# One image's preparation rotated over two image bodies by a table, and shifted copies made by DMA instead of VectorE

## The chip, the cores and the metric

The kernel runs on one core of one Trainium2 chip. The metric is the device time of one execution, in microseconds (us), median of the runs shown. The five engines are named as the profile names them: PE is TensorE (PEld its weight loads), DVE is VectorE, ACT is ScalarE, POOL is GpSimd, SP is SyncE, which here only issues DMAs.

## What is computed

The input is `x` of 32 images, 192 channels, 32 x 32 pixels, float32. Two residual branches follow each other.

```python
x = x + channel_attention(group_norm(x))     # 192 x 192 attention matrix per image, softmax, output product
h = group_norm(x)
offset = clip(conv3x3(h, off_w) + off_b, -8, 8)      # 2 x 9 taps
mask   = 2 * sigmoid(conv3x3(h, mask_w) + mask_b)    # 9 taps
y = deformable_conv3x3(h, offset, mask, proj_w) + proj_b   # bilinear, zero outside the image
x = x + gelu(batch_norm(y) * gamma + beta)   # mean and variance over all 32 images
```

## The kernel before

All images pass through one software pipeline. Work on an image has two parts, and every engine runs its own share of both, in program order, with semaphores between the engines.

The **body** of an image (`part1`) is 48 units, `for u in range(UNITS)`. In a unit PE does nine f16 matmuls into `acc` (`convolve`), five into `zps` for a unit ten further on (`z_group(u + AHEAD)`) and three float32 transposes into `sps` for the unit after next (`turn_s(u + 2)`). ACT copies `sps` and `zps` to f16 (`sh`, L890, and `zh`, L866), DVE forms the residues (`sl`, L1147, and `zl`, L1141), and POOL makes one `sT` tile for every two units (L1324). `sps` and `zps` have two buffers each, `sh`, `sl` and `sT` three. PE's `turn_s(v)` waits for the `sl` of v - 2, and so does `convolve`. Every twelve units PE adds `turn_y` and DVE `scale_y` (units 7, 19, ... of the body, the last after unit 47), every six ACT copies `acc`, and some units carry `y_stats` (DVE), `offset_distance` (DVE) and `column_hats` (ACT).

The **preparation** of an image (`part0`) is 48 stages, numbered 0 to 47, several of them empty. Stages 0 to 11 are statistics and the first normalisation: DVE `channel_stats` and `channel_moments` (0 to 2), `group_stats` on PE and `group_variance` on DVE (4), the power on POOL (5), four ACT normalisations (6 to 9), DVE `residue` (8 and 10). PE transposes in 12 to 15, 16 to 22 are the Gram matrix, the softmax and the products of the attention, 23 to 26 apply it and write `x1`, 27 to 29 are the second statistics, 30 to 33 four ACT normalisations into `x2`, 32 and 34 the DVE residues. Then come the copies that the 3 x 3 convolutions need:

```python
def move(k, b, par):                         # stages 33, 35 and 36, k = 0, 1, 2
    dve.tensor_copy(x2s[k] plane 0, columns 1.., <- x2 columns ..30)
    dve.tensor_copy(x2s[k] plane 1, columns ..30, <- x2 columns 1..)
    dve.tensor_copy(seam[:, 0:WRAP], src[:, H - WRAP:H])
    return dve.tensor_copy(seam[:, WRAP:2 * WRAP], src[:, 0:WRAP])
```

Stages 38 and 39 are PE's `offset_conv`, 108 matmuls each, 40 the offsets (DVE), 41 to 46 the vertical hats (DVE, ACT) and the first quarter of the horizontal hats (POOL, ACT). In the kernel before, stage u of image b + 1 stands at the end of unit u of image b on every engine; POOL, which goes by pairs of units, does stages 2p - 4 and 2p - 3 after tile p.

Image 0 is prepared alone, then image 0's body runs in straight-line code, then a hardware loop of 15 rounds with two images each, then image 31 without a preparation beside it. SP's queue holds, in order: for every image the store of `x1` and the load of the next `x` (`attended`, which waits for `x1`), and the store of `y` of the image before (`convolved`). A last phase reads `y` and `x1` back, applies the batch norm and stores the output.

Of the kernel before, what the change touches and what calls it, by code (L numbers as in the profile page):

```python
# [35 lines left out]
P = 128  # L36
# [46 lines left out]
def build(nc, x, w_qkT, w_v, w_outT, b_out, w_off, b_off, w_proj, proj_b, gamma, beta,  # L83
# [6 lines left out]
    with ExitStack() as ctx:  # L90
# [58 lines left out]

        x2s = [sb(f"x2s_{n}", [P, 2, PAD_ROWS * W], F16) for n in ("hi_a", "lo_a", "hilo_b")]  # L150

        x2w = [sb(f"x2w_{n}", [P, 2, 2 * WRAP * W], F16) for n in ("hi_a", "lo_a", "hilo_b")]

        x2 = [sb(f"x2_{n}", [P, 2, PAD_ROWS * W], F16) for n in ("hi_a", "lo_a", "hilo_b")]
        off = sb("off", [P, 2, TILES, J])
# [70 lines left out]
        x1_sb = sem("x1_sb")  # L226
        x1_stored = sem("x1_stored")
        x2_moved = sem("x2_moved")
        off_ps = sem("off_ps")
# [96 lines left out]
        def all_pairs(eng, step):  # L326
# [3 lines left out]
            for i in range(PAIRS - ROUND_ENDS):  # L330
                step(ROUNDS, i)

        def images(program, eng):

            part0, part1, weights_ready = program
            for u in range(SLOTS):
                part0(u, 0, 0)
                if u == 15:  # L340
                    weights_ready()
            part1(0, 0, True)
            with eng.Fori(1, NB - 2, 2) as b:
                part1(b, 1, True)
                part1(b + 1, 0, True)
            part1(NB - 1, (NB - 1) % 2, False)

        def image_alone(program, b, i):

            part0, part1, far_pass = program
            for u in range(SLOTS):
                part0(u, b, 0)
            part1(b, 0, False, i)
            far_pass(b, i)
# [58 lines left out]
        def _(sp):  # L415
# [30 lines left out]
            attended(0)  # L446
            with sp.Fori(1, NB - 2, 2) as b:
# [4 lines left out]
            attended(NB - 1, False)  # L452
            convolved(NB - 2)


# [18 lines left out]
            def image(b, i):  # L474
                load_x(i)
                sp.wait_ge(x1_sb, 4 * b + 4)
                store_x1(i)
                sp.wait_ge(y_final, b + 1)
                store_y(i)
# [34 lines left out]
        def _(pe):  # L514
# [227 lines left out]

            def part1(b, par, more, i=None):
                if first(b) or i is not None:
                    for g in range(AHEAD):
                        z_group(g, b, par)
                    turn_s(0, b)
                    turn_s(1, b)
                for u in range(UNITS):
                    if u + 2 < UNITS:  # L750
                        turn_s(u + 2, b)
                    elif more:
                        turn_s(u + 2 - UNITS, b + 1)
                    convolve(u, b, par)
                    if u == 9 and not more and i is None:
                        offset_max(b)
                    if u + AHEAD < UNITS:
                        z_group(u + AHEAD, b, par)
                    elif more:
# [13 lines left out]
        def _(act):  # L773
# [117 lines left out]

            def part1(b, par, more, i=None):
                if first(b) or i is not None:
                    for g in range(AHEAD):
                        split_z(g, b, par)
                    split_s(0, b)
                    split_s(1, b)
                for u in range(UNITS):
                    if u + 2 < UNITS:
                        split_s(u + 2, b)  # L900
                    elif more:
                        split_s(u + 2 - UNITS, b + 1)
                    if u % 12 == 4 and u < 36:
                        column_hats(u // 12 + 1, b, par)
                    if u % 6 == 5:
                        t = u // 6
                        act.wait_ge(sz_done, UNITS * b + u + 1)
                        if t >= 4 or not first(b):
                            act.wait_ge(yt_ps, 4 * b + t // 2 - 1)
                        act.copy(ypm[:, t % 4, 0:C], acc[:, 0:C])  # L910
                        act.copy(ypm[:, t % 4, C:2 * P], acc[:, P:C]).then_inc(y_pm, 1)  # L911
                    if u + AHEAD < UNITS:
                        split_z(u + AHEAD, b, par)
                    elif more:
                        split_z(u + AHEAD - UNITS, b + 1, 1 - par)
                    if more:
                        part0(u, b + 1, 1 - par)

# [17 lines left out]
        def _(dve):  # L936
# [64 lines left out]

            def move(k, b, par):

                rows = lambda v: v.rearrange("p (h w) -> p h w", w=W)
                src = rows(inner(x2[k], par))
                dve.tensor_copy(rows(inner(x2s[k], 0))[:, :, 1:W], src[:, :, 0:W - 1])
                dve.tensor_copy(rows(inner(x2s[k], 1))[:, :, 0:W - 1], src[:, :, 1:W])
                seam = rows(x2w[k][:, par])
                dve.tensor_copy(seam[:, 0:WRAP], src[:, H - WRAP:H])
                return dve.tensor_copy(seam[:, WRAP:2 * WRAP], src[:, 0:WRAP])  # L1010

            def zero_outside(hat, rows, tiles):
# [10 lines left out]
            def part0(u, b, par):  # L1023
# [55 lines left out]
                if u == 32:  # L1079
                    residue(0, inner(x2[1], par), inner(x2[0], par), 1, b)  # L1080
                if u == 33:
                    if not first(b):
                        dve.wait_ge(off_ps, b)
                    move(0, b, par)
                if u == 34:
                    residue(1, inner(x2[2], par)[CB:P], inner(x2[2], par)[CB:P], 1, b)
                if u == 35:
                    dve.wait_ge(xn_lo, 4 * b + 4)
                    move(1, b, par)
                if u == 36:  # L1090
                    move(2, b, par).then_inc(x2_moved, 1)
                if u == 40:
# [122 lines left out]

            def part1(b, par, more, i=None):
                if first(b) or i is not None:
# [4 lines left out]
                for u in range(UNITS):  # L1222
                    if u + 2 < UNITS:
                        split_s(u + 2, b)
                    elif more:
                        split_s(u + 2 - UNITS, b + 1)
                    if u + AHEAD < UNITS:
                        split_z(u + AHEAD, b, par)
                    elif more:
                        split_z(u + AHEAD - UNITS, b + 1, 1 - par)  # L1230
                    if u == 7 and i is None:
                        offset_distance(b, par)
                        if not more:
                            offset_flag_wanted()
                    if u == 11 and i is None and not more:
                        offset_flag()
                    if 5 <= u < 7 and i is None and not first(b):
                        y_stats(u - 3, b - 1, 1 - par)
                    if u in (38, 39) and i is None:
                        y_stats(u - 38, b, par)  # L1240
                    if u % 12 == 7 and u > 12:
                        scale_y(u // 12 - 1, b, par)
                    if more:
                        part0(u, b + 1, 1 - par)
                scale_y(3, b, par)
                if not more and i is None:
                    y_stats(2, b, par)
# [31 lines left out]
        def _(pool):  # L1279
            pool.memset(mhalf[:, :], -0.5)  # L1280
            pool.memset(minus[:, :], -1.0)
            for t in (*x2, *x2s):
                ins = pool.memset(t[:, :, :], 0.0)
            ins.then_inc(pool_setup, 1)
# [26 lines left out]

            def part1(b, par, more, i=None):
                for p in range(3 * TILES):
# [12 lines left out]
                    if p in (1, 4, 10):  # L1326
                        column_distance((1, 4, 10).index(p) + 1, b, par)
                    if more:

                        for u in (2 * p - 4, 2 * p - 3):  # L1330
                            part0(u, b + 1, 1 - par)

# [60 lines left out]
```

## Time and profile before

| | |
|---|---|
| time, median of 3 runs | 4050.97 us (4041.22 to 4051.61) |
| the profiled execution | 4042.66 us, span 4041.0 us |
| PE busy | 3563.3 us, 88% of the span |
| DVE busy | 2633.4 us, 65% |
| ACT busy | 2109.1 us, 52% |
| POOL busy | 1412.3 us, 35% |
| mean granted PE clock | 0.961 |

The body of image 0 begins at 122.8 us and that of image 31 ends about 3817 us. What lies behind it, some 220 us, is the last phase, which is bound by DMA and which the change doesn't touch. In a profile line the part in front of the bar is busy time, the part behind it idle time before the instructions and what ended it.

### The profile page before, as it was taken

To read this page: it belongs to the slowest core of one execution; us is meant where nothing else is said; L and a number is where in the kernel's file an instruction comes from. 1 tells how busy PE (TensorE), PEld (TensorE's weight loads), DVE (VectorE), ACT (ScalarE), POOL (GpSimd) and SP (SyncE) were. 2 spreads that over 40 slices of the span, in tenths; PEclk is the share of its full clock that TensorE was granted. 3 is DMA by queue.
4 is the path that set the end of the run, shared out by engine and by line. 5 is a ranking of instruction groups with operands and counts; after the bars stand their busy time and mean duration, and the time that the engine had idled before them with its cause. 6 is when DMAs were issued, how large, how long until landed. Compare 5 with 4: busy or idle time off the path is not lost.

```text
span 4041.0 us, 108743 instructions
## 1 busy us (share of the span) xinstructions
PE 3563.3 (88%) x38307; PEld 3052.9 (76%) x38307; DVE 2633.4 (65%) x5773; ACT 2109.1 (52%) x4790; POOL 1412.3 (35%) x1165
## 2 busy tenths in 40 slices
PE   3999999999999999999999999999999999999700
PEld 2788887888888788888878888887887878788700
DVE  3566776676667667676766766676666667766622
ACT  1555554555555455555545555555555555555432
POOL 1333333343433333333333333333333333333311
PEclk8999999999999999999999999999999999999955
DMA  2000000000000000000000000000001000000299
GB/s 63 20 10 28 29 28 20 28 28 18 20 28 28 20 28 28 28 10 28 28 21 28 28 28 10 29 28 28 20 28 28 28 11 28 28 20 18 69 374 322
DMA packets 50763, 170.48 MB, mean 42 GB/s; under 512 B 9665, under 2 KB 10881, under 8 KB 50177
## 3 DMA queue, kind: packets, MB, share of 16 engines
q1 hardware_dynamic: 39584, 136.75, 11.1%
q0 software_dynamic: 7168, 25.17, 1.6%
q8 instruction: 349, 5.72, 0.6%
q14 instruction: 238, 1.94, 0.2%
q10 hardware_dynamic: 3424, 0.90, 0.1%
HBM read 87.29 MB, written 75.50 MB: 40 GB/s over the span
## 4 chain that ended last, share of the span: by engine, by line
PE 62%; DVE 14%; issue 11%; ACT 5%; DMA 4%; DVEq 2%; ACTq 1%; SPq 1%; POOL 0%; POOLq 0%
PE sps L680 9%; PE acc L697 6%; PE acc L699 6%; PE acc L698 6%; PE l L609 4%; DVE zl L1141 3%; PE zps L666 3%; PE zps L670 3%; PE zps L667 3%; PE zps L668 3%; PE zps L669 3%; DVE sl L1147 2%; DMA xn<-x_scratch 2%; ACT sh L890 2%; DVE ych L1201 2%
## 5 line engine op out<-in xcount | busy, mean ns | idle before, releaser
L1324 POOL TENSOR_TENSOR sT<-ay,bx 128x768 f32<-128x768 f32 x768 | 1149.1, 1506 | 1400.8 <-PE sps L680 1333.5
L1147 DVE TENSOR_TENSOR sl<-sps,sh 128x384 f16<-128x384 f32 x1536 | 846.8, 551 | 597.9 <-ACT sh L890 595.0
L697 PE MATMUL acc<-zh,sh 128*128 128x192 f16 x4608 | 1139.7, 247 | 0.3 <-ACT ypm L911 0.3
L698 PE MATMUL acc<-zl,sh 128*128 128x192 f16 x4608 | 1139.7, 247 | 0.0
L699 PE MATMUL acc<-zh,sl 128*128 128x192 f16 x4608 | 1139.7, 247 | 0.0
L890 ACT CAST sh<-sps 128x384 f16<-128x384 f32 x1536 | 740.5, 482 | 728.4 <-PE sps L680 723.5
L866 ACT CAST zh<-zps 128x288 f16<-128x288 f32 x1536 | 619.7, 403 | 652.5 <-PE zps L670 625.5
L680 PE MATMUL sps<-eye,sT 128*128 128x128 f32 x4608 | 790.9, 281 | 155.7 <-DVE sl L1147 96.1
L1141 DVE TENSOR_TENSOR zl<-zps,zh 128x288 f16<-128x288 f32 x1536 | 693.4, 451 | 356.9 <-ACT zh L866 351.8
L680 PEld LDWEIGHTS sps<-eye,sT 128*128 128x128 f32 x4608 | 536.1, 142 | 308.5 <-DVE sl L1147 168.9
L698 PEld LDWEIGHTS acc<-zl,sh 128*128 128x128 f16 x4608 | 453.6, 98 | 18.5
L697 PEld LDWEIGHTS acc<-zh,sh 128*128 128x128 f16 x4608 | 453.5, 98 | 1.1 <-DVE sl L1147 0.5
L699 PEld LDWEIGHTS acc<-zh,sl 128*128 128x128 f16 x4608 | 453.5, 98 | 0.5
L666 PE MATMUL zps<-wpr_h,x_hi_a 128*128 128x288 f16 x1344 | 387.2, 288 | 1.2 <-DVE zl L1141 0.7
L667 PE MATMUL zps<-wpr_l,x_hi_a 128*128 128x288 f16 x1344 | 386.9, 288 | 0.0
L668 PE MATMUL zps<-wpr_h,x_lo_a 128*128 128x288 f16 x1344 | 386.4, 287 | 0.0
L669 PE MATMUL zps<-wpr_h,x_hilo_b 128*128 128x288 f16 x1344 | 385.8, 287 | 0.0
L670 PE MATMUL zps<-wpr_l,x_hilo_b 128*128 128x288 f16 x1344 | 385.7, 287 | 0.0
L1308 POOL TENSOR_TENSOR bx<-off,cx_sb 128x576 f32<-128x576 f32 x128 | 155.5, 1215 | 458.8 <-DVE off L1104 458.8
L1290 POOL TENSOR_TENSOR rstd<-gvar,mhalf 128x2 f32<-128x2 f32 x64 | 44.9, 702 | 563.5 <-DVE gvar L994 563.5
L609 PE MATMUL l<-wof,x2s_hi_a 128*128 128x54 f16 x1536 | 182.6, 186 | 9.8 <-DVE x2w_hilo_b L1010 9.8
L609 PE MATMUL l<-wof,x2s_lo_a 128*128 128x54 f16 x1536 | 182.5, 186 | 0.0
(201 smaller groups left out, 6466.3 us busy)
## 6 DMA issues: line engine op xcount, KB each, us to landing
xin<-in_x SPq DMA_DIRECT2D x32, 512.0 KB, 5.3
xin<-in_x SPq DMA_DIRECT2D x64, 256.0 KB, 5.9
x_scratch<-x SPq DMA_DIRECT2D x32, 512.0 KB, 2.8
y_scratch<-ych SPq DMA_DIRECT2D x32, 512.0 KB, 2.7
zh<-y_scratch SPq DMA_DIRECT2D x20, 512.0 KB, 10.9
zl<-x_scratch SPq DMA_DIRECT2D x20, 512.0 KB, 12.4
out<-zh POOLq DMA_DIRECT2D x20, 512.0 KB, 8.8
x_scratch<-x SPq DMA_DIRECT2D x32, 256.0 KB, 3.5
```

Of the source, the lines that this page charges most:

```text
L609: mm = pe.matmul(o, src[:, row * W:(row + ROWS_T) * W], wof[:, m, k].rearrange("p i j -> p (i j)"), start=(k == 0 and n == 0), stop=(k == ...
L666: pe.matmul(o, at(0), wpr_h[:, 0, ky, n], start=True, stop=False)
L667: pe.matmul(o, at(0), wpr_l[:, 0, ky, n], start=False, stop=False)
L680: mm = pe.transpose(sps[u % 2][:, kx * P:(kx + 1) * P], sT[:, g, kx, c * P:(c + 1) * P], eye32[:, :])
L697: pe.matmul(acc[:, 0:C], s_h, zh[:, j, ky, z], start=start and kx == 0, stop=False)
L698: pe.matmul(acc[:, 0:C], s_h, zl[:, j, ky, z], start=False, stop=False)
L699: mm = pe.matmul(acc[:, 0:C], s_l, zh[:, j, ky, z], start=False, stop=stop and kx == 2)
L866: act.copy(z_piece(zh, g, par), zps[:, g % 2, 0:KO // 2]).then_inc(z_hi, 1)
L890: act.copy(sh[:, u % S_RING].rearrange("p k n -> p (k n)"), sps[u % 2][:, 0:3 * P]).then_inc(s_hi, 1)
L1141: dve.tensor_tensor(z_piece(zl, g, par), zps[:, g % 2, 0:KO // 2], z_piece(zh, g, par), ALU.subtract)\
L1147: dve.tensor_tensor(one(sl), sps[u % 2][:, 0:3 * P], one(sh), ALU.subtract).then_inc(s_lo, 1)
L1324: pool.tensor_tensor(sT[:, p % ST_RING].rearrange("p k (r x) -> p k r x", r=R), a, x_, ALU.mult)\
```

## The change

1. The three planes of `x2`, `x2s` and `x2w` become one tile each, with the plane as a dimension.
2. DVE's `move` goes (twelve copies per image). SP issues four SBUF-to-SBUF DMAs in its place (`shift`), each of 128 partitions x 3 planes: two of 96 elements (192 bytes) per run, two of 1023 elements (2046 bytes) per run. The planes are now shifted as a flat row, and POOL clears the column that wrapped (`edges`, two memsets in stage 37), which releases PE's `offset_conv` and, for the next body, `z_group`.
3. A table `PLAN` says in which unit each stage stands. Stages 0 to 18 of image b + 2 stand in units 30 to 47 of image b, stages 19 to 46 of image b + 1 in units 0 to 29 of image b. Between stage 34 (unit 16) and stages 35 to 37 (unit 20) there are three units without a stage. Image 0's body takes the whole of image 1's preparation in 38 units and stages 0 to 18 of image 2 in the last ten.
4. The loop has 14 rounds, and images 29, 30 and 31 stand behind it.
5. `column_hats` moves from units 4, 16, 28 to 4, 14, 22, `offset_distance` from 7 to 17, `y_stats` from 5, 6, 38, 39 to 2, 3, 35, 37.

```diff
+        PLAN = {-18: (0,), -17: (1,), -16: (2,), -15: (3,), -14: (4,), -13: (5,),
+                -12: (6,), -11: (7,), -10: (8,), -9: (9,), -8: (10, 11), -7: (12,), -6: (13,), -5: (14,), -4: (15,),
+                -3: (16,), -2: (17,), -1: (18,), 0: (19,), 1: (20,), 3: (21,), 4: (22,), 5: (23,), 6: (24,),
+                7: (25,), 8: (26,), 9: (27,), 10: (28,), 11: (29,), 12: (30,), 13: (31,), 14: (32,), 15: (33,),
+                16: (34,), 20: (35, 36, 37), 21: (38,), 22: (39,), 23: (40,), 24: (41,), 25: (42,), 27: (44,),
+                28: (45,), 29: (46,)}
+        LEAD = -min(PLAN)
+        FIRST_UNITS = UNITS - 10
+        def squeezed(units, span, offset):
+            out = {}
+            for at in range(span):
+                out.setdefault(offset + at * units // span, []).extend(PLAN.get(at - LEAD, ()))
+            return out
+        FIRST_PLAN = squeezed(FIRST_UNITS, LEAD + max(PLAN) + 1, 0)
+        FIRST_LEAD = squeezed(UNITS - FIRST_UNITS, LEAD, FIRST_UNITS)
+        def beside(part0, u, b, par, left):
+            if left >= 1:
+                for stage in FIRST_PLAN.get(u, ()) if first(b) else PLAN.get(u, ()) if u >= 0 else ():
+                    part0(stage, b + 1, 1 - par)
+            if left >= 2:
+                for stage in FIRST_LEAD.get(u, ()) if first(b) else PLAN.get(u - UNITS, ()):
+                    part0(stage, b + 2, par)
...
-            with eng.Fori(1, NB - 2, 2) as b:
+            with eng.Fori(1, NB - 4, 2) as b:
...
+            def shift(b, par):
+                sp.wait_ge(xn_lo, 4 * b + 4)
+                plane = x2_all[:, :, par, PAD_T * W:PAD_T * W + N]
+                flat_plane = lambda h: x2s_all[:, :, h, PAD_T * W:PAD_T * W + N]
+                sp.dma_start(x2w_all[:, :, par, 0:WRAP * W], plane[:, :, N - WRAP * W:N]).then_inc(x2_shifted, 16)
+                sp.dma_start(x2w_all[:, :, par, WRAP * W:2 * WRAP * W], plane[:, :, 0:WRAP * W])\
+                  .then_inc(x2_shifted, 16)
+                sp.dma_start(flat_plane(0)[:, :, 1:N], plane[:, :, 0:N - 1]).then_inc(x2_shifted, 16)
+                sp.dma_start(flat_plane(1)[:, :, 0:N - 1], plane[:, :, 1:N]).then_inc(x2_shifted, 16)
...
             with sp.Fori(1, NB - 2, 2) as b:
                 attended(b)
+                shift(b, 1)
                 convolved(b - 1)
                 attended(b + 1)
+                shift(b + 1, 0)
                 convolved(b)
...
-                if u == 33:
-                    if not first(b):
-                        dve.wait_ge(off_ps, b)
-                    move(0, b, par)
...
-                if u == 35:
-                    dve.wait_ge(xn_lo, 4 * b + 4)
-                    move(1, b, par)
-                if u == 36:
-                    move(2, b, par).then_inc(x2_moved, 1)
...
+                if u == 37:
+                    edges(b)
...
+            def edges(b):
+                pool.wait_ge(x2_shifted, 64 * b + 64)
+                pool.sem_inc(edges_due, 1)
+                for h in range(2):
+                    rows = x2s_all[:, :, h, PAD_T * W:PAD_T * W + N].rearrange("p k (r w) -> p k r w", w=W)
+                    ins = pool.memset(rows[:, :, :, (W - 1) * h:(W - 1) * h + 1], 0.0)
+                ins.then_inc(x2_moved, 1)
...
-                    if more:
-                        part0(u, b + 1, 1 - par)
+                    beside(part0, u, b, par, left)
```

## Rows read from the trace of the kernel before

**Rows 1.** The page: busy time by engine; the SP queue: packets, MB, share of 16 engines.

```profile
PE 3563.3 (88%) x38307; PEld 3052.9 (76%) x38307; DVE 2633.4 (65%) x5773; ACT 2109.1 (52%) x4790; POOL 1412.3 (35%) x1165
...
q1 hardware_dynamic: 39584, 136.75, 11.1%
```

**Rows 2.** One instruction per image (stage 40): duration, first and last start in us.

```profile
L1097 DVE SCALAR_TENSOR_TENSOR off<-l,unscale,boff x32: 431/433/443, 106.4 to 3729.1; 128x216 f32<-128x216 f32 x32
```

**Rows 3.** Waits of PE from 320 to 3720 us: total us, times, longest.

```profile
PE sps L680 <- DVE sl L1147: 91.3, 119, 1.1
PE sps L680 <- issue: 48.4, 14, 3.7
PE l L540 <- DVE gram L1057: 17.4, 29, 0.6
```

**Rows 4.** PE's timeline, the transposes of `turn_s` in units 33 to 37: start, us.

```profile
2066.95 0.49 PE L680 MATMUL sps<-eye,sT 128*128 128x128 f32 x3
2068.64 0.49 PE L680 MATMUL sps<-eye,sT 128*128 128x128 f32 x3
2070.61 0.55 PE L680 MATMUL sps<-eye,sT 128*128 128x128 f32 x3
2073.59 0.55 PE L680 MATMUL sps<-eye,sT 128*128 128x128 f32 x3 [1.08 <-DVE sl L1147]
2075.80 0.55 PE L680 MATMUL sps<-eye,sT 128*128 128x128 f32 x3 [0.31 <-DVE sl L1147]
```

**Rows 5.** DVE's timeline over the same units.

```profile
2068.38 1.72 DVE L1000 TENSOR_TENSOR x_lo_a<-xn,x_hi_a 128x1024 f16<-128x1024 f32 x1
...
2071.53 1.45 DVE L1009 COPY x2w_hi_a<-x_hi_a 128x96 f16<-128x96 f16 x1
...
2073.93 1.22 DVE L1000 TENSOR_TENSOR x_hilo_b<-xn,x_hilo_b 64x1024 f16<-64x1024 f32 x1
```

**Rows 6.** POOL's timeline over the same units.

```profile
2071.24 1.69 POOL L1324 TENSOR_TENSOR sT<-ay,bx 128x768 f32<-128x768 f32 x1 [2.23 <-PE sps L680]
```

**Rows 7.** ACT's timeline, `sh` before and behind the normalisation of stage 31.

```profile
2065.23 0.47 ACT L890 CAST sh<-sps 128x384 f16<-128x384 f32 x1
...
2067.02 0.48 ACT L890 CAST sh<-sps 128x384 f16<-128x384 f32 x1
```

**Rows 8.** PE's timeline, the transposes that end units 9, 10 and 11.

```profile
2007.47 0.49 PE L680 MATMUL sps<-eye,sT 128*128 128x128 f32 x3
2009.45 0.55 PE L680 MATMUL sps<-eye,sT 128*128 128x128 f32 x3
2011.19 0.49 PE L680 MATMUL sps<-eye,sT 128*128 128x128 f32 x3
```

**Rows 9.** DVE's timeline, the residue of stage 10.

```profile
2010.94 1.70 DVE L1000 TENSOR_TENSOR xhl_b<-xn,xhl_b 64x1024 f16<-64x1024 f32 x1
```

**Rows 10.** PE's timeline, units 42 to 44, 46, and `turn_y` in 47.

```profile
2093.40 0.49 PE L680 MATMUL sps<-eye,sT 128*128 128x128 f32 x3
2095.86 0.55 PE L680 MATMUL sps<-eye,sT 128*128 128x128 f32 x3 [0.61 <-DVE sl L1147]
2097.86 0.55 PE L680 MATMUL sps<-eye,sT 128*128 128x128 f32 x3
...
2101.33 0.49 PE L680 MATMUL sps<-eye,sT 128*128 128x128 f32 x3
2103.26 0.32 PE L710 MATMUL yt<-eye,ypm 128*128 128x128 f32 x1
```

**Rows 11.** Groups by line, ACT: one half of `column_hats`.

```profile
L857 ACT ACTIVATE bx<-bx 128x576 f32<-128x576 f32 x128 | 88.5, 691 | 0.1
```

**Rows 12.** Groups by line, DVE: one half of `scale_y`.

```profile
L1201 DVE TENSOR_SCALAR ych<-yt,unscale,pb 128x256 f32<-128x256 f32 x256 | 126.2, 534 | 2.3 <-PE yt L711 2.3
```

**Rows 13.** DMA issues: KB each, median us from issue to landing.

```profile
xin<-in_x SPq DMA_DIRECT2D x64, 256.0 KB, 5.9
x_scratch<-x SPq DMA_DIRECT2D x32, 512.0 KB, 2.8
```

More of the change, by code:

```diff
@@ L148, in build @@
         rinv = sb("rinv", [P, 2])
-        x2s = [sb(f"x2s_{n}", [P, 2, PAD_ROWS * W], F16) for n in ("hi_a", "lo_a", "hilo_b")]
-        x2w = [sb(f"x2w_{n}", [P, 2, 2 * WRAP * W], F16) for n in ("hi_a", "lo_a", "hilo_b")]
-        x2 = [sb(f"x2_{n}", [P, 2, PAD_ROWS * W], F16) for n in ("hi_a", "lo_a", "hilo_b")]
+        x2s_all = sb("x2s", [P, 3, 2, PAD_ROWS * W], F16)
+        x2w_all = sb("x2w", [P, 3, 2, 2 * WRAP * W], F16)
+        x2_all = sb("x2", [P, 3, 2, PAD_ROWS * W], F16)
+        x2s, x2w, x2 = [[t[:, k] for k in range(3)] for t in (x2s_all, x2w_all, x2_all)]
         off = sb("off", [P, 2, TILES, J])
@@ L477, in image @@
                 store_x1(i)
+                shift(b, 0)
                 sp.wait_ge(y_final, b + 1)
@@ L741, in far_pass, with part1 @@
                     mm.then_inc(fyt_ps, 1)
-            def part1(b, par, more, i=None):
+            def part1(b, par, left, i=None):
                 if first(b) or i is not None:
@@ L751, in part1 @@
                         turn_s(u + 2, b)
-                    elif more:
+                    elif left:
                         turn_s(u + 2 - UNITS, b + 1)
                     convolve(u, b, par)
-                    if u == 9 and not more and i is None:
+                    if u == 9 and not left and i is None:
                         offset_max(b)
@@ L758, in part1 @@
                         z_group(u + AHEAD, b, par)
-                    elif more:
+                    elif left:
                         z_group(u + AHEAD - UNITS, b + 1, 1 - par)
@@ L900, in part1 @@
                         split_s(u + 2, b)
-                    elif more:
+                    elif left:
                         split_s(u + 2 - UNITS, b + 1)
-                    if u % 12 == 4 and u < 36:
-                        column_hats(u // 12 + 1, b, par)
+                    if u in (4, 14, 22):
+                        column_hats((4, 14, 22).index(u) + 1, b, par)
                     if u % 6 == 5:
@@ L913, in part1 @@
                         split_z(u + AHEAD, b, par)
-                    elif more:
+                    elif left:
                         split_z(u + AHEAD - UNITS, b + 1, 1 - par)
-                    if more:
-                        part0(u, b + 1, 1 - par)
+                    beside(part0, u, b, par, left)
             images((part0, part1, lambda: None), act)
@@ L1000, in residue @@
                 dve.tensor_tensor(lo, xn[:, 0] if i == 0 else xn[CB:P, 1], hi, ALU.subtract).then_inc(xn_lo, 1)
[L1002 to L1010, printed above, removed]
             def zero_outside(hat, rows, tiles):
@@ L1214, in y_stats, with part1 @@
                     ins.then_inc(y_final, 1)
-            def part1(b, par, more, i=None):
+            def part1(b, par, left, i=None):
                 if first(b) or i is not None:
@@ L1224, in part1 @@
                         split_s(u + 2, b)
-                    elif more:
+                    elif left:
                         split_s(u + 2 - UNITS, b + 1)
@@ L1228, in part1 @@
                         split_z(u + AHEAD, b, par)
-                    elif more:
+                    elif left:
                         split_z(u + AHEAD - UNITS, b + 1, 1 - par)
-                    if u == 7 and i is None:
+                    if u == (17 if left else 7) and i is None:
                         offset_distance(b, par)
-                        if not more:
+                        if not left:
                             offset_flag_wanted()
-                    if u == 11 and i is None and not more:
+                    if u == 11 and i is None and not left:
                         offset_flag()
[L1237 to L1240, printed above, removed]
+                    if u in (2, 3) and i is None and not first(b):
+                        y_stats(u, b - 1, 1 - par)
+                    if u in (35, 37) and i is None:
+                        y_stats((u - 35) // 2, b, par)
                     if u % 12 == 7 and u > 12:
                         scale_y(u // 12 - 1, b, par)
-                    if more:
-                        part0(u, b + 1, 1 - par)
+                    beside(part0, u, b, par, left)
                 scale_y(3, b, par)
-                if not more and i is None:
+                if not left and i is None:
                     y_stats(2, b, par)
@@ L1281, in _ @@
             pool.memset(minus[:, :], -1.0)
-            for t in (*x2, *x2s):
-                ins = pool.memset(t[:, :, :], 0.0)
+            for t in (x2_all, x2s_all):
+                ins = pool.memset(t[:, :, :, :].rearrange("p k h n -> p (k h n)"), 0.0)
             ins.then_inc(pool_setup, 1)
@@ L1327, in part1 @@
                         column_distance((1, 4, 10).index(p) + 1, b, par)
-                    if more:
-                        for u in (2 * p - 4, 2 * p - 3):
-                            part0(u, b + 1, 1 - par)
+                    for u in (2 * p - 4, 2 * p - 3):
+                        beside(part0, u, b, par, left)
+                for u in range(UNITS - 4, UNITS):
+                    beside(part0, u, b, par, left)
             images((part0, part1, lambda: None), pool)
```

20 lines of the change are left out of this document (13 added, 7 removed).

## The prediction

> **What bounds the kernel now.** I read the page first: PE is busy 88% of the span, DVE 65% [rows 1], so the body of the images is PE's, and a gain must be PE time that is not work. Stage 40 comes once per image, from 106.4 to 3729.1 us over 31 intervals: 116.9 us per image [rows 2]. The waits of PE in the steady stretch are few: the transposes of `turn_s` wait for DVE's `sl`, 3.1 us per image; 14 waits of some 3.5 us are for nothing but issue, one at each turn of the loop; and one product of stage 21 waits 0.6 us for DVE [rows 3].
>
> A wait in that list is counted short, because the last matmul's end covers its beginning. So I measure from start to start. A quiet unit takes 1.68 us (two `turn_s` in a row are 1.69 apart), and then come 1.97, 2.98 and 2.21 us [rows 4]; the next unit, with `move(1)`, repeats the 2.98. These four units lie where stages 33 to 36 stand. The surplus is 0.29 + 1.30 + 0.53 + 1.30 = 3.4 us per image, the largest stall outside the loop turn.
>
> The reader should see why. DVE's seam copy of 96 elements takes 1.45 us [rows 5] and ends at 2072.98, with the POOL tile that began at 2071.24 and took 1.69 (to 2072.93) [rows 6]: the copy sat behind POOL. By the Trainium skill ("SBUF — State Buffer", section Terms) DVE and GpSimd share a port pair that is locked for a full instruction; the trace agrees, and the sum is the same with or without that rule. In the same way the residue of stage 34 is 1.22 us and that of stage 32 1.72 us [rows 5].
>
> **How much lateness is free.** `turn_s(v)` needs the `sl` of v - 2, so an `sl` may be about one unit, 1.68 us, later than in a quiet unit before PE stands still; PE work that lies between (a `turn_y`, a stage) adds to that. ACT has its own: with a normalisation in the unit one `sh` follows the other by 1.79 us [rows 7], 0.11 more than a unit, so four in a row are just affordable. These two facts size every new collision below.
>
> **The change, part by part.** Per image beside which a full preparation runs:
>
> *The moves go*: -3.4. Their wait behind POOL goes too. DVE is then idle in the units that held them.
>
> *Stage 21* is now two units behind stage 20 instead of one: the product's wait goes. It is 0.6 idle; corrected as above (1.08 idle [rows 4] against 1.30 by starts) about -0.75.
>
> *Stages 8 to 12.* Before, the unit that follows the residue of stage 8 takes 1.98 us [rows 8], 0.30 over; in the new place a `turn_y` (some 0.4 us of PE work) lies there and hides it: -0.3. But stage 12 follows stage 10 by one unit instead of two. The residue of stage 10 ends at 2012.64 [rows 9]; one unit earlier PE would come to its transposes at about 2011.2 [rows 8]. PE would wait 1.4 us; if the residue runs without POOL's tile in its way, in 1.22 as stage 34's, 0.9. Bounds 0.9 and 1.5, I take +1.4. Behind the waiting transposes all of PE is queued.
>
> *Stages 41 to 46.* Before, two units take 2.46 and 2.00 [rows 10], 1.1 over, since ACT's hats hold up `sh`. A `turn_y` now falls in the first of them: -0.4, the rest stays. Stage 46's unit has no `turn_y` behind it any more and body unit 47 has stage 18 in front of its own: the 0.25 by which `turn_y` waited (2103.26 - 2101.33 - 1.68) [rows 10] go. `column_hats` at 22 lies beside stage 39, a long PE unit; at 4 beside stage 22, likewise. Both at nothing, and 0.5 if that cover failed.
>
> *column_hats in unit 14* lies among the four normalisations. It adds 2 x 0.69 = 1.4 us of ACT [rows 11] to an `sh` already 1.1 late (the interval of 1.79 [rows 7] less `sh` and `zh` themselves, an estimate), less 0.4 for the `turn_y` of unit 14: 2.1 against a free 1.68 is a stall of 0.45, and with the residue of stage 32 [rows 5] queued on DVE behind it up to 1.0, of which 0.3 were there before. Net +0.1 to +0.7; I take +0.4, as DVE's part depends on POOL's timing.
>
> *scale_y in unit 31* now lies before stages 1 and 2 and puts 2 x 0.53 us [rows 12] in front of the moments for which PE's stage 4 waits. DVE had some 0.6 us to spare per unit (1.68 less a `sl` and a `zl`). 0 to 1.06, I take +0.45.
>
> *The transfer.* SP is free at unit 16 (the `x1` store and `x` load go out at unit 8, the `y` store at unit 3), so nothing is queued behind `shift` for ten units. The four DMAs move 2 x 786 KB and 2 x 74 KB, 1.72 MB. The SP queue moved 136.75 MB in 11.1% of sixteen engines' time over 4041 us [rows 1], that is 305 KB/us with all sixteen busy. A 512 KB store lands in 2.8 us [rows 13], of which 1.7 would be data: 1.1 fixed. So 1.1 + 5.6 = 6.7 us. From below: at the store's own whole rate less a fixed 1.5, 400 KB/us, 5.8. From above: three loads, 1.05 MB, the last issued about 1.5 us behind the first and landing 5.9 later [rows 13], 7.4; scaled, 11.4. I take 6.7, nearer the stores since nothing is read from HBM. `edges` on POOL adds about 0.5 (an estimate; no row shows so small a strided memset; under the 1.69 of a whole tile [rows 6]). Together 7.2. What covers it: from the residue's end, about 2.3 us into unit 17 counted on DVE's lag (the 1.22 of [rows 5] behind its `zl`), to `offset_conv` at the end of unit 21: some 3.3 units, 5.6 us. PE waits +1.6 us; bounds 0.7 and 6.3. POOL waits too, in program order, with tile 12 done: tile 13 is needed at unit 24, behind both `offset_conv`, so that wait costs nothing below some 8 us more.
>
> By the Trainium skill ("DMA: Bandwidth & Descriptors", section Anatomy of one DMA, a fit for the path over GpSimd) a DMA takes about 2.0 us + bytes/436 KB per us; that estimate would be 5.9 us and 0.8 less stall. The same page of the Trainium skill (section Specifications) wants 512 B for line rate, which speaks against the 192-byte seam runs; doubling their 0.15 MB would add about half a microsecond. No run so far shows either for SBUF to SBUF.
>
> *Sum per image*: removed 3.4 + 0.75 + 0.3 + 0.4 + 0.25 = 5.1; added 1.4 + 0.4 + 0.45 + 1.6 = 3.85. Net -1.25 us, times about 29 = -36.
>
> *Once*: one loop turn fewer, -3.5, and less slow PE after it. In the preparation of image 0 nothing hides the transfer: 7.2 against the moves behind its second residue, about 2.5: +5. Image 0's body packs 48 + 18 stages into 48 units: in its last ten units two stages of a chain share a unit six times, and 35 to 38 share one four units behind 34 instead of five. At one to two us for each that is about +13. The fewer rounds leave more straight-line code; at nothing, since the trace shows no issue wait on entering or leaving the loop.
>
> *Total*: -36 - 3.5 + 5 + 13 = -21 against the profiled 4042.7: 4021. The median of the runs is 0.2% above the profiled time, which would make it 4030; I forecast 4026, between the two.
>
> **The rivals.**
>
> *B, more is hidden.* The transfer lands in 5.8 and the planes' residues run at 1.22: no wait at unit 21 (-1.6) and 0.5 less at unit 41. For it: everything at the quick end is in a row above. Against it: it needs the cover of 5.6 to hold. -2.1 x 29 = -61: about 3965.
>
> *C, the transfer is slow: slower than before.* 384 runs per DMA instead of 128, shifted by two bytes, could go at the loads' pace. With 11.4 us `offset_conv` starts 4.7 us later: +136, about 4160. It decides from where the net gain is gone: 25 us over 29 images is 0.9, so from about 7.6 us for the four DMAs; by 0.3% slower from 8.0. Waits of over 3 us would also be like the loop turns', of which the mean granted clock of 0.961 has its share. Midway, 9 us, gives about 4095.
>
> *D, crowding.* Every unit now has a stage, and DVE and ACT are late more often than my list has it. One more us per image: about 4055, no change.
>
> **How the numbers follow.** A, my forecast, 4026 with its own range 3995 to 4050: 0.40. B, 3940 to 3995: 0.22. C, over 4063: 0.23. D, 4040 to 4063: 0.15. A measurement of this kernel can tell 0.3%, 12 us, from no change: faster is below 4039. Faster: 0.36 of A, B and a little of D, 0.6; same: the rest of A and D, 0.16; slower 0.24. The range 3945 to 4100 leaves out the ends of B and C.
>
> **What would show it.** No DVE copies at the old lines; in units 16 to 20 `turn_s` 1.68 apart; PE's stage 38 waiting for POOL's memset 1 to 2 us, and 5.8 to 7.5 us from the first of SP's four DMAs to the last landing; PE's stage 12 waiting 1 to 1.5 for DVE's residue; `turn_s` in units 14 to 17 at most 1 us late; stage 40 every 115.6 us. Wrong if the DMAs take over 8 us, if stage 12 finds its residue done, or if image 0's body takes over 20 us more than the 117 or so of the others.

## The result: slower by 3.3%

The changed kernel takes 4181.95 us (median of 4 runs, 4178.28 to 4185.12) against 4051.29 us: a ratio of 1.033, 95% interval 1.031 to 1.035. One of the four runs behind the 4051.29 is a slow one of 4744.94 us, which the ratio leaves out; without it the median is the 4050.97 given above. Forecast were 4026 us and a range up to 4100. In the profiled execution the span is 4176.2 us against 4041.0.

The page of the changed kernel, busy time by engine and the SP queue, and its stage 40 once per image (answers to [rows 1, 2]):

```profile
PE 3591.9 (86%) x38307; PEld 3083.9 (74%) x38307; DVE 2482.4 (59%) x5389; ACT 2098.3 (50%) x4790; POOL 1413.4 (34%) x1225
...
q1 hardware_dynamic: 90784, 191.76, 14.6%
```
```profile
L1124 DVE SCALAR_TENSOR_TENSOR off<-l,unscale,boff x32: 432/433/443, 109.3 to 3821.9; 128x216 f32<-128x216 f32 x32
```

DVE lost 151 us of work, as the change meant it to, and PE is busy for a smaller share: the gain on DVE was not PE's. PE's waits from 320 to 3720 us (total, times, longest), beside [rows 3]:

```profile
PE l L657 <- POOL x2s L1338: 81.2, 29, 3.3
PE sps L728 <- DVE sl L1174: 55.6, 114, 1.2
PE sps L728 <- issue: 53.8, 26, 2.6
PE l L601 <- DVE xhl_b L1046: 37.8, 28, 1.4
```

The first line is the wait for the transfers and POOL's `edges`, 2.8 us per image, and it is new. So is the fourth, stage 12 behind the residue of stage 10, 1.35 us. The waits for `sl` fell from 3.1 to 2.0 us, not to nothing. One wait for the transfers in time, on SP, POOL and PE:

```profile
2122.51 0.69 SPq L479 DMA_DIRECT2D x2w<-x  x1
...
2124.61 0.64 SPq L483 DMA_DIRECT2D x2s<-x  x1
```
```profile
2129.72 0.93 POOL L1338 MEMSET x2s<- 128x96 f16 x2 [8.50 <-DMA x2s<-x]
```
```profile
2130.71 0.32 PE L657 MATMUL l<-wof,x2s 128*128 128x54 f16 x3 [2.32 <-POOL x2s L1338]
...
2134.93 0.53 PE L728 MATMUL sps<-eye,sT 128*128 128x128 f32 x3
...
2136.64 0.24 PE L657 MATMUL l<-wof,x2s 128*128 128x54 f16 x3
...
2139.37 0.53 PE L728 MATMUL sps<-eye,sT 128*128 128x128 f32 x3
```

SP issues the four one after the other, 0.7 us each, so the two large ones (`x2s`) are issued 1.4 and 2.1 us behind the first. From the first issue to POOL's start it is 7.2 us, and 8.2 to PE's.

This is the shorter of two kinds, which alternate from image to image: of the 29 waits 14 are 2.3 us long and 14 are 3.3. In the longer kind, as behind the first issue at 2246.52, POOL starts 8.2 us behind it, and the DMA view of 2246.5 to 2255 us has one packet of instructions among those of the four transfers:

```profile
2254.70 0.93 POOL L1338 MEMSET x2s<- 128x96 f16 x2 [9.47 <-DMA x2s<-x]
```
```profile
q14 instruction: 1, 0.01, 0.2%
```

The same view of 2122.5 to 2130 has none. It is like that in every run that kept this order of the transfers: without such a packet the four land in 7.0 to 7.5 us, with one in 7.1 to 9.2, most often about 8.0. No run changes this packet alone, so that it is the cause is likely and not shown.

Now compare the two halves of the convolution, 108 matmuls each: the first takes 4.2 us (2130.71 to 2134.93), the second 2.7 (2136.64 to 2139.37). The same image by stretches (busy us of PE, PEld, DVE, ACT and POOL, granted PE clock, DMA share, GB/s):

```profile
2128.40:2130.70 2.30, 0.00 (x0) 0.00 (x0) 0.46 (x1) 0.40 (x1) 0.98 (x3) 1.00 0.32 124
2130.70:2135.00 4.30, 4.29 (x109) 4.29 (x110) 0.00 (x0) 0.00 (x0) 2.57 (x2) 0.60 0.01 4
2135.00:2141.00 6.00, 6.00 (x146) 5.75 (x143) 1.49 (x3) 2.75 (x7) 0.00 (x0) 1.00 0.01 3
```

Behind 2.3 us without a matmul PE was granted 0.60 of its clock, that is 1.2 GHz instead of 2.4 for most of the stretch. It fell so behind 20 of the 29 waits, 9 of the 14 short ones and 11 of the 14 long ones. Before the change it fell, in this stretch of 320 to 3720 us, only behind the loop's turn.

To see where the rest went I took the start of each of the 48 units from the trace and compared its mean over images 2 to 28 with a unit of the same content that has no stall. What stands over, us per image, before and after:

| place | before | after | forecast of the difference |
|---|---|---|---|
| the moves, units 35 to 37 | 3.1 | 0 | -3.4 (with unit 34) |
| stage 21 | 0.9 | 0.1 | -0.75 |
| offset convolution: wait and slow clock | 0.1 | 3.9 | +1.6 |
| stages 8 to 12 | 0.5 | 1.9 | +1.1 |
| four normalisations, residues (16 to 18; before 34) | 0.3 | 1.2 | +0.4 |
| stages 41 to 46 | 1.2 | 2.0 | -0.4 |
| stage 4 | 0.2 | 0.7 | +0.45 |
| loop turn and slow clock behind it | 2.7 | 3.2 | 0 |
| stage 28, `turn_y` in 47 | 0.9 | 0.6 | -0.25 |
| all | 9.9 | 13.6 | -1.25 |

Measured whole, a body takes 117.0 us before and 120.6 after, and the bodies of images 1 to 29 together 100 us more. The turn's share rose because PE now waits twice there, 4.1 us in all, where it waited once for 3.5. Once per execution: image 0's body takes 143.9 us instead of 114.1, of which 10 are work that image 30 no longer has (104.0 instead of 114.3), so +20; the preparation of image 0 +3; the last phase +12. The last is not the change's: in the padded kernel before (below) it takes 236 us, as in the changed one, against 224 in the profile of before.

### The profile page after: what moved, and what is told of

Read it like the earlier page. It is cut to its first block, busy times and chain, and to the rows that moved or that the text cites. A ratio compares the mean times of both kernels' runs of the same rounds, so it can differ in the third digit from the quotient of the medians.

```text
span 4176.2 us, 107654 instructions
## 1 busy us (share of the span) xinstructions
PE 3591.9 (86%) x38307; PEld 3083.9 (74%) x38307; DVE 2482.4 (59%) x5389; ACT 2098.3 (50%) x4790; POOL 1413.4 (34%) x1225
## 4 chain that ended last, share of the span: by engine, by line
PE 57%; DVE 13%; issue 10%; DMA 8%; ACT 5%; SPq 2%; DVEq 2%; ACTq 2%; POOL 1%; POOLq 0%
PE sps L728 8%; PE acc L745 5%; PE acc L746 5%; PE acc L747 5%; PE l L657 5%; DMA x2s<-x 4%; PE zps L718 3%; PE zps L714 3%; PE zps L715 3%; PE zps L716 3%; PE zps L717 3%; DVE zl L1168 2%; DMA xn<-x_scratch 2%; DVE x L1046 2%; DVE sl L1174 2%
## 5 line engine op out<-in xcount | busy, mean ns | idle before, releaser
L1361 POOL TENSOR_TENSOR sT<-ay,bx 128x768 f32<-128x768 f32 x768 | 1137.5, 1492 | 1343.8 <-PE sps L728 1340.2
L728 PE MATMUL sps<-eye,sT 128*128 128x128 f32 x4608 | 791.7, 281 | 118.8 <-DVE sl L1174 61.2
L728 PEld LDWEIGHTS sps<-eye,sT 128*128 128x128 f32 x4608 | 545.6, 142 | 210.8 <-DVE sl L1174 108.9
L714 PE MATMUL zps<-wpr_h,x 128*128 128x288 f16 x1344 | 386.7, 288 | 0.4
L718 PE MATMUL zps<-wpr_l,x 128*128 128x288 f16 x1344 | 386.6, 288 | 0.0
L715 PE MATMUL zps<-wpr_l,x 128*128 128x288 f16 x1344 | 386.6, 288 | 0.0
L716 PE MATMUL zps<-wpr_h,x 128*128 128x288 f16 x1344 | 386.6, 288 | 0.0
L717 PE MATMUL zps<-wpr_h,x 128*128 128x288 f16 x1344 | 386.6, 288 | 0.0
L657 PE MATMUL l<-wof,x2s 128*128 128x54 f16 x4608 | 214.7, 194 | 105.9 <-POOL x2s L1338 105.9
L657 PEld LDWEIGHTS l<-wof,x2s 128*128 128x128 f16 x4608 | 197.6, 102 | 117.0 <-POOL x2s L1338 115.4
```

The costliest lines, as they stand in the source:

```text
L657: mm = pe.matmul(o, src[:, row * W:(row + ROWS_T) * W], wof[:, m, k].rearrange("p i j -> p (i j)"), start=(k == 0 and n == 0), stop=(k == ...
L714: pe.matmul(o, at(0), wpr_h[:, 0, ky, n], start=True, stop=False)
L715: pe.matmul(o, at(0), wpr_l[:, 0, ky, n], start=False, stop=False)
L728: mm = pe.transpose(sps[u % 2][:, kx * P:(kx + 1) * P], sT[:, g, kx, c * P:(c + 1) * P], eye32[:, :])
L1361: pool.tensor_tensor(sT[:, p % ST_RING].rearrange("p k (r x) -> p k r x", r=R), a, x_, ALU.mult)\
```

## The experiments

Each is compared with the kernel before on the same chip; ratios carry their 95% interval. The kernel before took 4041 to 4047 us beside the experiments and 4051 beside the changed kernel, so a difference of under some 10 us between two groups of experiments says little by itself. Numbers per unit are taken as for the table.

**The two halves of the change.** First the transfers alone, with `PLAN` = `{u: (u,)}` and hats, `offset_distance` and `y_stats` in their old units.

> The four transfers and POOL's edges as in the change, but every stage, column_hats, offset_distance and y_stats back in their old units (stage u in unit u). Theory (the wait for the transfers, and the slow clock behind it, is the largest part of the loss): the cover is about 4 us here for 8.2 us from the residue's end to the edges, so PE waits about 4 us in unit 38 and its offset convolution runs about 1.5 us longer; the moves' 3.1 us are saved. +2.5 us per image, about 4125 us. Rival (the new places of the stages cost, the transfers are hidden): 3.1 us less per image than before, about 3960 us.

4183.1 us, 1.0335 (1.0318 to 1.0353). The direction is the theory's, the size is 58 us more. Its largest wait of PE:

```profile
PE zps L709 <- POOL x2s L1333: 150.1, 28, 6.3
```

5.4 us per image, and not at the convolution: `z_group` of the next image also waits for `x2_moved`, and with the stages in their old units it comes first in unit 38. I had overlooked it. With the slow clock, unit 38 is 7.2 us over. Another 7 us that the expectation left out come once per execution, in the preparation of image 0, where no body hides the transfers.

Then the table alone: `move(0)` to `move(2)` back on DVE in units 15, 17 and 18, without `shift` and `edges`.

> The table with DVE's copies in place of transfers and edges: move(0) in unit 15, move(1) in 17, move(2) in 18. Theory: the wait in unit 21 goes (-3.8 us per image against the change), the moves' stall comes back (3.1 to 4 us), the other new stalls and the long first body stay: 4165 to 4190 us, as slow as the change. Rival (the transfers are the whole loss): the table by itself is neutral, about 4050 us.

4129.2 us, 1.020 (1.018 to 1.022): better than the 4165 to 4190 expected. The moves in their new places stall PE by 2.9 us and not 3.1 to 4, and without transfers the preparation and the body of image 0 take 12 us less, which the expectation left out; some 20 us of the difference stay open. But it is 82 us slower than before. So each half alone makes the kernel slower; the transfers are not the whole loss.

**The wait.** Stages 35 to 46 two units later:

```diff
-16: (34,), 20: (35, 36, 37), 21: (38,), 22: (39,), 23: (40,), 24: (41,), 25: (42,), 27: (44,), 28: (45,), 29: (46,)}
+16: (34,), 22: (35, 36, 37), 23: (38,), 24: (39,), 25: (40,), 26: (41,), 27: (42,), 29: (44,), 30: (45,), 31: (46,)}
```

> The change with stages 35 to 46 two units later, which gives the transfers 3.4 us more cover. Theory: the wait of 2.3 to 3.3 us in front of the offset convolution and the slow clock behind it go, up to 0.5 us per image comes back where stages 44 to 46 now meet stages 0 and 1: -3.3 us per image, about 4085 us. Rival (the wait only stands in for DVE's and ACT's lateness, which would stall PE elsewhere): within 15 us of 4182.

4068.7 us, 1.005 (1.003 to 1.007): 113 us gained by 3.4 us more cover. PE no longer waits for `x2s`. First in its list is now

```profile
PE sps L723 <- DVE sl L1169: 60.8, 145, 1.2
```

then issue (57.8 us in 26 waits), stage 12 as in the changed kernel (39.2 in 29) and stage 4 (13.8 in 29, 7.8 in the changed kernel).

The offset convolution no longer stands over by anything, 3.9 us per image gained, 0.6 given back at stages 0 to 4. That is the rival's end: apart from these 0.6 us, lateness did not reappear elsewhere.

**The slow clock.** Useless work in the wait:

```diff
+ pe.wait_ge(gn_var, 2 * b + 2)
+ for n in range(11):
+     pe.matmul(l0[0][:, :], eye16[:, :], wpr_h[:, 0, 0, 0:512], start=True, stop=True)
  pe.wait_ge(x2_moved, b + 1)
```

> The change with eleven matmuls of 512 columns (2.3 us, into a bank that nobody reads then) in front of PE's wait for the edges; they fill the wait and add no needed work. Theory (the idle stretch drops the granted clock, and the offset convolution pays 1.2 to 1.5 us for it): -1.2 us per image, about 4147 us, and the mean granted clock rises from 0.947 to about 0.96. Rival (the longer convolution has another cause, or the clock drops anyway): 4182 us or a little above.

4108.0 us, 1.015 (1.013 to 1.017), clock 0.963: 74 us gained by adding work, twice what was expected. I looked where. The convolution's unit gained 0.5 us: of its 3.4 us over, 2.3 are the added matmuls and 1.0 a rest of waiting, so next to nothing is left of the 1.1 us of slow clock. (Added work and rest of the wait are together 0.5 us longer than the wait was, which is why the unit gained 0.5 and not the 1.1.) The larger gain, 1.9 us per image, lies at the loop's turn:

```profile
PE l L660 <- POOL x2s L1341: 27.9, 29, 2.1
PE sps L731 <- issue: 21.7, 13, 2.1
```

The turn waits once (13 times) for 1.7 us; in the changed kernel twice (26), 4.1 us together. Neither theory had that; it is taken up below.

**The order of the transfers.** The two `x2s` DMAs issued ahead of the two `x2w`.

> The change with the two large transfers issued before the two small ones. Theory (SP's four issues of 0.7 us in a row put the large ones 1.4 us late, and the last large one ends the wait): the edges come about 1 us sooner, PE's wait in unit 21 falls from 2.8 to about 1.8 us and the slow clock behind it (1.1 us) in part: -1 to -2 us per image, 4125 to 4150 us. Rival (the data time of all four sets the end, whatever the order): 4182 us.

4142.9 us, 1.025 (1.022 to 1.027): 39 us gained, as the theory had it. The wait at the convolution is 61.2 us in 28 instead of 81.2 in 29, 0.6 us less each, and with the clock the unit stands over by 1.5 us less: the clock fell behind 4 of the 28 waits instead of 20 of 29, behind none of the 14 of 1.75 us and behind 4 of the 14 of 2.6. The issues cost SP more in this order, 1.3 and 1.4 us for the two small ones.

**Stage 12.** Stages 0 to 11 one unit earlier.

> The change with stages 0 to 11 one unit earlier, so that stage 12 is two units behind the residue of stage 10 again. Theory: the 1.5 us that PE waits there per image go, nothing else moves by more than 0.4 us: 4140 us. Rival (DVE's and ACT's lateness there is paid in the next units anyway): within 15 us of 4182.

4140.7 us, 1.024 (1.021 to 1.027): 41 us, as expected. The 1.9 us of stages 8 to 12 are gone and 0.3 more stand at stage 4. Another 0.5 stand at the convolution, whose waits are the same: here the clock fell behind all 29 of them.

**column_hats in unit 16**: `if u in (4, 16, 22)`.

> The change with the second column_hats in unit 16 instead of 14, behind the last of the four normalisations. Theory (1.4 us of ACT among the four normalisations is what stalls units 16 to 18 by 1.24 us): about 0.9 us less per image, 4156 us. Rival (the residues on DVE set that stall, as they did before the change): 4182 us, within 10.

4190.2 us, 1.0355 (1.033 to 1.038): no gain. The 8 us more can't be told from nothing by the times alone, but in the trace a body takes 0.5 us more. Units 16 to 18 stand over by 1.8 us instead of 1.2. The theory holds for units 16 and 17, which gain 0.3 us, and misses unit 18, which loses 0.9: out of the way of the normalisations the hats meet ACT's copy of `acc` in unit 17, for which PE then waits too (8.4 us in 28).

**Together**, these three and the later offsets:

> The three of this call and the two units more of cover, together. If the stalls are separate, as the theory has it: 4069 of the run with the later offsets less 43 for stage 12 and 26 for column_hats, the order of transfers then hidden: about 4000 us, faster than before the change by 1.2%. Rival (lateness only moves on to the next tight place): 4050 us or more.

4065.7 us, 1.005 (1.003 to 1.006). 3 us under the later offsets alone. Part is the hats' loss, part a new meeting: with stages 44 to 46 in units 29 to 31 and stages 0 to 2 one unit earlier, DVE's moments come late and unit 33 stands over by 1.6 us; and image 0's body, which now holds 19 units' worth of the next preparation, takes 146.5 us against 139.2 with the later offsets alone.

> Later offsets, stage 12 later and planes first together, column_hats back in unit 14. From the combined run's 4066 less the 0.6 us per image that unit 16 cost (its units 16 to 18 stalled 1.83 us against 1.24): 4048 us, the same as before the change. If it is nearer 4030, the loss of the combined run lay in the hats' place alone.

With the hats back in unit 14: 4044.8 us, 1.0006 (0.9992 to 1.0020). The mended table costs no time and gains none.

**The place of the loop's code.** 64 matmuls of two columns on PE in the preparation of image 0; the loop is the same.

```diff
  pe.wait_ge(dve_setup, 3)
+ for n in range(64):
+     pe.matmul(acc[:, 0:2], eye16[:, :], wpr_h[:, 0, 0, 0:2], start=True, stop=True)
```

> The run above with 64 two-column matmuls more on PE in the preparation of image 0, where PE waits anyway: only the place of the loop's code moves. Theory (the turn of the loop costs PE more or less by where the loop's code lies against the blocks in which it is fetched; 4.1 us of issue waits per turn in the changed kernel, 1.7 with the added matmuls, 3.5 before): the wait per turn changes by over 0.5 us, the time by 7 to 30 us. Rival (the busier PE or the clock shortened the turn in the run that was busy while waiting): within 5 us of the run above, 4.1 us per turn.

3995.3 us, 0.988 (0.985 to 0.991): 49 us, more than expected. Two other tables, without padding:

> As e9, with image 0's body giving 34 units to image 1's preparation and 14 to the first stages of image 2 (38 and 10 before). Theory (two stages of a chain in one unit cost PE their latency, and the last ten units have most of them): the first body falls by 3 to 8 us, the time by as much. Rival (the pressed transfer in that body costs as much as is won): no change.

4039.7 us, 0.9995 (0.998 to 1.001). The first body fell by 3.2 us to 143.3, which the times can't tell from nothing.

> As e9 with stages 35 to 46 three units later instead of two. DVE's stage 42 then comes between POOL's tiles instead of beside one, as before the change. Theory (the 1.62 us that stage 42's product takes is its wait for POOL's tile, 0.46 otherwise): 0.9 us less in the units behind it, but stages 44 to 46 then stand beside stages 1 to 3: 4025 to 4048 us. Rival (the collision with stages 1 to 3 costs more): over 4048.

4054.2 us, 1.003 (1.002 to 1.004): the rival's side. Stages 41 to 46 stand over by as much as two units later, at ACT's copy of `acc` instead (36 us of waits), and units 32 and 33 by 0.4 more. But the run does not test the theory, since it did not do what it was made for: the product of stage 42 still takes 1.62 us in it.

Then the kernel before and the changed kernel with the same padding:

> The kernel before with the 64 added matmuls ahead of its loop. Its turn waits 3.5 us once (13 turns of the version with the later offsets wait twice, 4.1 to 4.4 us together). If the place of the code decides, the wait per turn changes here too, to between 1.7 and 4.4 us: 4010 to 4055 us. If the added matmuls' gain was peculiar to the table, no change.

> The same with 128. By the theory of place it gives another wait than 64 does; by the rival both equal the kernel before within 0.3%.

4044.4 and 4045.6 us, 1.0001 (0.998 to 1.002) and 1.0006 (0.999 to 1.002). No change; the wait stays at 3.4 to 3.5 us per turn.

> The changed kernel with the 64 matmuls: how much of its 131 us of loss is the turn of its loop. The theory of place: -45 to -50 us as with the mended table, about 4134 us, and the rest of the loss stays (wait and slow clock in unit 21, stage 12, first body). Rival (the place explains the loss): 4060 us or less.

4163.5 us, 1.031 (1.028 to 1.033). The turn gained what it gained elsewhere (24.8 us of issue waits instead of 53.8), but the wait for the transfers is longer, 99.4 us instead of 81.2, and all 29 waits are now over 3 us. In the changed kernel every second image had no packet of instructions among its transfers; here all 29 have one, of 16 KB in those images. So the place takes some 41 us off the turns and puts some 20 on the convolution. Net, of the loss of 131 us, it explains 19 by the times and 9 by the ratios.

> The best parts together: later offsets, stage 12 later, planes first, 34 units in the first body, 64 matmuls. 3995 of the padded run less 4: about 3990 us.

4001.4 us, 0.990 (0.987 to 0.993), 11 over the expectation and no better than the padded run without the 34 units: image 0's body takes 146.0 us here, so nothing was gained there.

> The mended table of e9 with 16 added matmuls instead of 64. If the place of the loop's code against a boundary decides, 16 may fall on either side: two issue waits per turn and 4.1 us (about 4045 us), or one and 1.8 us (about 3996). Any third value speaks for something gradual.

> The same with 128. A boundary gives again one of the two values, 4045 or 3996 us, with 26 or 13 issue waits. If the added matmuls helped as such (by what PE did before), it would be 3996 or less.

16 give 4000.1 us, 0.988 (0.986 to 0.991); 128 give 4046.9, 1.0005 (0.999 to 1.002). Of four paddings (none, 16, 64, 128) two give one value and two the other, and not in the order of the number. PE's issue waits of the mended table from 320 to 3720 us, without padding, with 16 and with 128:

```profile
PE sps L723 <- issue: 58.0, 26, 2.9
```
```profile
PE sps L725 <- issue: 23.0, 13, 2.2
```
```profile
PE sps L725 <- issue: 55.8, 26, 2.9
```

That the place of the code decides between two waits at the turn and one is shown. By what mechanism is not: the page counts 360 or 361 instruction packets of 16 KB with two waits and 347 with one, but 362 in the kernel before with 64, against 349 without and 350 with 128, and there the wait did not change. Nor does the count give the length: the transfers alone have 347 and one wait per turn, of 3.3 us.

## Why the prediction was wrong

**What failed first: the term of the transfers**, "PE waits +1.6 us". The mechanism, the place and the cover were right: DVE's residue ended 5.9 us before PE came (5.6 forecast). The size was not. Four DMAs took 7.1 and 8.0 us in turn instead of 6.7. I had counted one start-up of 1.1 us and then data at 305 KB/us. Both parts were off, in opposite ways: the issues come one by one, 0.7 us each, and the large transfers are in full flow only 2.6 us behind the first issue, but then they move faster:

```profile
2125.10:2129.20 4.10, 3.29 (x34) 2.79 (x32) 3.27 (x8) 2.11 (x5) 0.00 (x0) 1.00 0.99 383
```

That is 4.1 us for the 1.57 MB of the two, where my rate gives 5.2. In every second image some 0.9 us come on top, together with a packet of instructions, of which I had no term. By an estimate from the Trainium skill ("DMA: Bandwidth & Descriptors", section Anatomy of one DMA) the four would take 5.9; the trace doesn't agree with its 7.1 and 8.0, and the measurement decides. `edges` took 0.9 instead of 0.5. Together 8.2 and 9.2 for 7.2, less a cover of 5.9: waits of 2.3 and 3.3 us, 2.8 in the mean, for the 1.6 of the forecast.

**What was left out: the clock.** 1.1 us per image in the mean. I had written that waits of over 3 us would be like the loop turn's and given them no price; 2.3 us could be enough. Not by their length alone: behind waits of 2.3 us the clock fell 9 times of 14 in the changed kernel, 14 of 14 with stage 12 later and once of 14 with the hats in unit 16. What else decides stays open. The clock makes a shorter wait worth more than its length: the run with planes first gives back 1.5 us for 0.6 of wait. Wait and clock as forecast 1.6, measured 3.8: 2.2 x 29 = 64 of the 156 us between forecast and result.

**Stages 41 to 46**: forecast 0.4 less, measured 0.8 more, 35 us in all; the 0.25 of `turn_y` in unit 47 came as forecast. I counted ACT's hats and moved them as they stood. But the stages changed from one kind of unit to the other: POOL makes a tile for every two units, and an operation of DVE that met POOL idle in stage 42 now meets its tile. Below are DVE and POOL (three tiles in a row) while PE is in unit 27, where 1.4 of the 2.0 us stand over, and the same product's durations before (least, median, most):

```profile
2147.81 1.62 DVE L1146 TENSOR_TENSOR ay<-ay,mask 128x288 f32<-128x288 f32 x1
```
```profile
2144.55 4.57 POOL L1361 TENSOR_TENSOR sT<-ay,bx 128x768 f32<-128x768 f32 x3
```
```profile
L1119 DVE TENSOR_TENSOR ay<-ay,mask x64: 457/660/1793, 109.4 to 3740.8; 128x288 f32<-128x288 f32 x64
```

The product of stage 42 takes 1.62 us here, that of stage 46, in unit 30 with POOL idle, 0.46. Before the change it was the other way round, 0.46 and 1.78. It looks like the wait of [rows 5, 6]: I had read it there, and did not ask where each DVE operation would stand against POOL after the move. How much of the 1.2 us is due to it no run tells apart.

**Stages 8 to 12** were sized right at stage 12 (1.4 forecast, 1.35 idle): a run that gave it back its unit gained 41 us. But the `turn_y` did not hide the 0.3 before it: the residue of stage 8 now takes 2.15 us (L1046) instead of 1.71.

**The normalisations**: forecast 0.4, measured 0.9, above the +0.7 that I had given as the upper end; the experiment says that moving the hats is no cure. Two slips are in that term. The 0.3 of unit 34 was taken off twice, in the 3.4 of the moves and again as "0.3 were there before". And 1.79 less `sh` and `zh` (0.48 and 0.40) is 0.9, not 1.1. **Stage 4** 0.45 and 0.5, **stage 21** -0.75 and -0.8, **the moves** 3.1 in three units and 0.3 in the one before: right. The **loop's turn**, forecast unchanged per turn, costs 0.5 us more per image. The **first body** 20 us for 13; two units of the table share one of its last ten eight times, not six.

Of the signs by which the forecast was to be known as wrong one came, the body of image 0: 143.9 us, 23 over the 120.6 of the others. Stage 40 came every 119.8 us and not every 115.6, PE's stage 38 waited 2.3 and 3.3 us and not 1 to 2, and units 16 and 18 took 2.21 us and not 1.68.

Rival C, slow transfers, is the case that came, though not by slow data: four issues in a row, a packet of instructions in every second image, a longer `edges` and the clock. Its price, 4.7 us for 11.4 us of transfer, would have needed a transfer that never came. D, crowding, came too: the table without transfers is 2% slower. I had given them 0.23 and 0.15, and treated them as alternatives; they added up.

The mended version (later offsets, stage 12 later, planes first, 16 or 64 matmuls of padding) is 1.2% faster than the kernel before, and as much against the padded ones. Only its loop's code lies well: without padding it is level.

## What to carry to other kernels

A wait on the bound engine has a second price when the granted clock falls behind it; from the idle length in the trace at which that happened elsewhere one cannot conclude that a shorter one is free. Where a stage moves, ask for each of its operations which tile of POOL it will stand beside, not only how long it was: the same product took 0.46 or 1.62 us. And when a loop is rewritten, measure it with some padding ahead of it before crediting or blaming the edit: the same loop came out at 4045 or at 4000 us.

## What the runs showed that I had not expected

- Eleven useless matmuls of 512 columns per image made the changed kernel 74 us faster; 0.5 us per image of that came from the convolution's unit, where the granted clock had fallen, the rest from the loop's turn.
- A turn of the changed loop costs PE 1.7 to 1.9 us in one issue wait or 4.1 to 4.5 us in two; 16 or 64 tiny matmuls ahead of the mended table's loop give the first, none or 128 the second. In the kernel before it is 3.4 to 3.5 in one wait with 0, 64 and 128, and 3.3 in one with the transfers alone.
- Four transfers of together 1.72 MB landed within 7.5 us where no packet of instructions fell among theirs, and within up to 9.2 us where one did.
- An issue of a DMA of 128 partitions with three runs each takes SP 0.63 to 0.69 us. Issued behind the two large ones, the two small ones take it 1.3 and 1.4 us.
- The granted clock fell behind 9, 14 and 1 of 14 waits of 2.3 us in three tables, behind 4 of 14 of 2.6 us in a fourth, and behind none of the 14 of 1.75 us there.
- The last phase, bound by DMA, takes 224 to 240 us with the same instructions in different executions. What decides it stays open.
